# Edge stage on one core: counting every 16th key and gathering key groups, and the feed-forward output stored by channel

## The reference

```
h = (x_flat @ W_gat).reshape(M, HEADS, NUM_EXPERTS)
src = jnp.concatenate([edge_index[0], loops])
dst = jnp.concatenate([edge_index[1], loops])
e = jax.nn.leaky_relu(a_src[src] + a_dst[dst], negative_slope=0.2)
e_max = jax.ops.segment_max(e, dst, num_segments=M)
ee = jnp.exp(e - e_max[dst])
denom = jax.ops.segment_sum(ee, dst, num_segments=M)
alpha = ee / (denom[dst] + 1e-16)
msg = h[src] * alpha[:, :, None]
agg = jax.ops.segment_sum(msg, dst, num_segments=M)
...
for ei in range(NUM_EXPERTS):
    g = jnp.where(topk_i == ei, w, 0.0).sum(-1)
    hh = jax.nn.gelu(x @ W1[ei] + b1[ei], approximate=False)
    out = out + g[..., None] * (hh @ W2[ei] + b2[ei])
```

## Time and profile before

| | us |
|---|---|
| median of 3 runs | 5598.91 |
| lowest, highest | 5587.48, 5601.15 |
| profiled execution: span (the profile gives no other time of its own for it) | 6624.5 |
| first gather of the edge phase starts | 2448.2 |
| last gather starts | 6150.2 |
| finish phase starts | 6343.5 |

### The profile page before, as it was taken

How to read it: one execution, slowest core, us unless ns; L and a number is a source line. 1 busy time by engine, 2 the same in 40 slices (tenths; PEclk the granted TensorE clock), 3 DMA queues, 4 the chain that set the end, 5 groups by cost and what they waited for, 6 DMA issues and landing times. The chain is left out here.

```text
span 6624.5 us, 60648 instructions
## 1 busy us (share of the span) xinstructions
PE 3002.6 (45%) x16592; PEld 2109.7 (32%) x16592; DVE 3002.1 (45%) x4301; ACT 1456.9 (22%) x5679; POOL 2970.5 (45%) x3274
## 2 busy tenths in 40 slices
PE   2888888869999760000444241311313130130620
PEld 1445455458888650000233120200202120120410
DVE  5888888649999731010899120110101011010358
ACT  0334343348888510000000010000000000010110
POOL 1000000026667537777000657575675757667045
PEclk9788888769999855555555555555555555555555
DMA  6566556646666450000000011110111111011143
GB/s 141 87 95 96 94 94 95 95 75 102 101 104 103 87 146 8 8 7 8 3 3 3 10 37 25 34 28 14 45 15 34 25 34 28 14 45 15 58 166 118
DMA packets 583690, 381.06 MB, mean 58 GB/s; under 512 B 404996, under 2 KB 524852, under 8 KB 577748
## 3 DMA queue, kind: packets, MB, share of 16 engines
q1 hardware_dynamic: 384376, 216.58, 14.6%
q10 hardware_dynamic: 89403, 109.89, 9.4%
q0 software_dynamic: 109728, 52.69, 6.7%
HBM read 232.80 MB, written 145.29 MB: 57 GB/s over the span
## 5 line engine op out<-in xcount | busy, mean ns | idle before, releaser
L1569 POOL DMA_INDIRECT e_row<-scratch_table,e_edge x2048 | 2014.2, 983 | 989.2 <-issue 680.8
L1750 PE MATMUL f_psY<-f_w,f_hid 128*128 128x64 f32 x1568 | 363.0, 425 | 1657.4 <-ACT f_hid L1701 1292.2
L1633 DVE TENSOR_TENSOR f_y<-f_psY,f_b 128x1024 f32<-128x1024 f32 x49 | 59.8, 1219 | 2298.5 <-DMA scratch_t<-t 1711.2
L1750 PEld LDWEIGHTS f_psY<-f_w,f_hid 128*128 128x128 f32 x1568 | 342.5, 330 | 1753.4 <-ACT f_hid L1701 1371.8
L1608 DVE TENSOR_TENSOR i_hot<-f_psH,i_digit 128x1024 bf16<-128x1024 f32 x512 | 582.3, 1211 | 640.0 <-DMA scratch_parts<-h2p 356.8
L1701 ACT ACTIVATE f_hid<-f_psH,f_b 128x512 f32<-128x512 f32 x196 | 131.4, 687 | 2933.9 <-PE f_psH L1745 1351.7
L1733 PE MATMUL f_psH<-i_hot 128*128 128x128 bf16 x2048 | 264.8, 310 | 958.3 <-DVE i_hot L1608 761.2
L964 POOL MEMSET a_wproj<- 128x128 f32 x1 | 0.2, 210 | 1367.4 <-POOLq L161 1367.4
L1077 ACT ACTIVATE prob<-psS,low 128x100 f32<-128x100 f32 x1568 | 514.1, 373 | 61.9 <-DVE low L1110 61.9
L1733 PEld LDWEIGHTS f_psH<-i_hot 128*128 128x128 bf16 x2048 | 197.3, 140 | 1025.7 <-DVE i_hot L1608 825.7
L472 PE MATMUL psH<-h,c_w 128*128 128x448 f32 x1008 | 511.5, 595 | 3.8 <-ACT h L584 2.0
(11 more groups left out here) (281 smaller groups left out, 5329.9 us busy)
## 6 DMA issues: line engine op xcount, KB each, us to landing
stack<-scratch_parts ACTq DMA_DIRECT2D x504, 112.0 KB
e_row<-scratch_table,e_edge POOLq DMA_INDIRECT x2048
scratch_y<-f_y ACTq DMA_DIRECT2D x49, 512.0 KB
scratch_state<-e_state SPq DMA_DIRECT2D x16, 1536.0 KB, 6.0
g_y<-scratch_y SPq DMA_DIRECT2D x24, 1024.0 KB
val<-scratch_vpad SPq DMA_DIRECT2D x672, 35.0 KB
scratch_parts<-h2p ACTq DMA_DIRECT2D x56, 336.0 KB, 3.3
keys<-scratch_kpad SPq DMA_DIRECT2D x112, 155.0 KB
```

What stands on the lines that cost most here:

```text
L1569: pool.indirect_dma_start(out=row[s][:, f, :], out_offset=None, in_=table_dram, in_offset=bass.IndirectOffsetOnAxis(ap=edge[s][:, 0, f:f + ...
L1750: m = pe.matmul(psY[par][:, j, e * C:(e + 1) * C], hid[e][:, j * 128:(j + 1) * 128], w2[:, e, :], start=True, stop=True)
```

## The change

- **The count.** Only every 16th key of the sorted list is counted (`GROUP` = 16, 128 columns instead of 2048), which tells in which group of 16 keys a node's run ends. POOL then fetches that group for each node with 128 indirect DMAs of 16 keys (`group_keys`), and DVE compares the 16 keys with the node's number and adds up. `Index` writes 128 digit columns instead of 2048; `digit` shrinks from 2 MB to 128 KB.
- **The order on POOL.** Three chunks of gathers, the 128 key-group gathers, chunk 3, the run starts, then chunks 4 to 15. The store of the first elements moves from POOL to SP.
- **The ring.** Eight row buffers and edge buffers instead of four. The one-hot tiles lie in the eighth row buffer, the fetched keys in `part`, their floats in `state[0]`. All loops of the phase are written out.
- **The feed-forward.** The second layer loads the weights, widened with zeros to 128 columns, and streams the hidden tile: 4 matmuls of 512 columns per tile, two experts added in one PSUM bank half each. ACT moves the result out of PSUM with the bias, one tile behind the gelus, and it is stored by channel. DVE has no part in it. It starts when the base of the count is out of PSUM (`freed`). ACT's list has the exponential of chunk c behind tile `EXPS_AFTER[c]`.
- **The finish.** The slices come in by channel; PE turns them with 16 transposes each into PSUM (`g_psM`, two buffers), and DVE scales from there. The token loads have a semaphore of their own.

```diff
-AHEAD = 4
+AHEAD = 8
+KEYS_BEFORE, RUNS_BEFORE = 3, 4
+EXPS_AFTER = (14, 15, 16, 17, 18, 22, 25, 29, 33, 36, 40, 44, 47, 49, 49, 49)
...
-            dve.tensor_scalar(part_i[:], dst[:], 127, None, ALU.bitwise_and).then_inc(self.done, 1)
+            dve.tensor_scalar(group, lasts, 127, None, ALU.bitwise_and).then_inc(self.done, 1)
...
+                def group_keys():
+                    pool.wait_ge(grouped, 1)
+                    for t in range(128):
+                        pool.indirect_dma_start(out=keys[:, t, :], out_offset=None, in_=key_rows,
+                                                in_offset=bass.IndirectOffsetOnAxis(ap=group_ix[:, t:t + 1], axis=0)).then_inc(keys_in, 16)
...
+                for c in range(NFC):
+                    if c == KEYS_BEFORE:
+                        group_keys()
+                    if c == RUNS_BEFORE:
+                        first_of_run()
+                    gather(c)
...
+                dve.tensor_copy(group_ix[:], inc[:]).then_inc(grouped, 1)
+                done(dve.memset(base[:], 0.0))
+
+                dve.wait_ge(keys_in, 16 * 128)
+                done(dve.tensor_scalar(keys, keys, SRC_BITS, NODES - 1, ALU.logical_shift_right, ALU.bitwise_and))
+                done(dve.tensor_copy(keyf, keys))
+                dve.wait_ge(const_in, 48)
+                done(dve.tensor_tensor(keyf, keyf, node_id[:].unsqueeze(2).to_broadcast([128, 128, GROUP]), ALU.is_le))
+                done(dve.tensor_reduce(inside[:], keyf, AX.X, ALU.add))
...
+                def outputs(t):
+                    wait(act, y_out[t % 2], t // 2 * 16)
+                    for a in range(2):
+                        act.wait_ge(y_ready, t * 2 + a + 1)
+                        m = act.activation(y[t % 2][:, a, :], psY[t % 2][:, a, :], ACT.Identity, bias=b2[:, a:a + 1])
...
-                        for j in range(ZT // 128):
-                            m = pe.matmul(psY[par][:, j, e * C:(e + 1) * C], hid[e][:, j * 128:(j + 1) * 128], w2[:, e, :],
-                                          start=True, stop=True)
...
+                        m = pe.matmul(psY[par][:, e // 2, :], w2[:, e, :], hid[e][:], start=e % 2 == 0, stop=e % 2 == 1)
...
-                    dve.tensor_tensor(scaled[k % 2][:, 0:n], y[s][:, 0:n], gate[:, lo:hi, :].unsqueeze(3).to_broadcast([128, n, EXPERTS, C]),
+                    dve.tensor_tensor(scaled[k % 2][:, 0:n], psM[k % 2][:, 0:n], gate[:, lo:hi, :].unsqueeze(3).to_broadcast([128, n, EXPERTS, C]),
...
+                def turn(k):
+                    s, (lo, hi) = k % SLOTS, CHUNKS_AT[k]
+                    pe.wait_ge(y_in[s], loads(k))
+                    wait(pe, scale_done, k - 1)
+                    for j in range(hi - lo):
+                        for a in range(2):
+                            m = pe.transpose(psM[k % 2][:, j, 2 * a:2 * a + 2, :].rearrange("p e c -> p (e c)"),
+                                             y[s][:, a, j * 128:(j + 1) * 128], ident[:])
+                    m.then_inc(y_turned, 1)
```

More of the change, by code:

```diff
@@ L1227, in step @@
             dve.wait_ge(self.done, 5)
-            dve.tensor_copy(out[:, :, 5, :], chunks(part_i)).then_inc(self.digits, 1)
+            dve.tensor_copy(self.digit[:, 1, :], group).then_inc(self.digits, 1)
         elif i == 7:
@@ L1464, in edge_phase @@
         b_first = sb("e_b_first", [128, GHEADS])
[L1465 to L1468, removed]
+        iota = sb("i_iota", [128, 128]); before = sb("i_before", [128, 128]); node_id = sb("i_node_id", [128, 128])
+        digit = sb("i_digit", [128, 2, FC])
         zero = sb("i_zero", [128, 128], BF16)
@@ L1480, in edge_phase @@
         part = sb("e_part", [128, FC, GH])
-        w1 = sb("f_w1", [C, EXPERTS, 128]); b1 = sb("f_b1", [128, EXPERTS]); w2 = sb("f_w2", [128, EXPERTS, C])
-        b2 = sb("f_b2", [128, EXPERTS * C])
+        zeros = e0
+        keys = part[:].bitcast(I32)
+        keyf = state[0][:, :, 0:GROUP]
+        spare = row[AHEAD - 1][:].rearrange("p f c -> p (f c)").bitcast(BF16)
+        hot = [[spare[:, (2 * i + d) * HOT * 128:(2 * i + d + 1) * HOT * 128].rearrange("p (c x) -> p c x", x=128) for d in range(2)] for i in range(2)]
@@ L1527, in _ @@
                 for c in range(NFC):
[L1528 to L1532, removed]
+                    sp.dma_start(flat[c], zeros[:].rearrange("p f h -> p (f h)")).then_inc(b_zeroed, 16)
@@ L1537, in _ @@
+                sp.wait_ge(b_started, 16)
                 for par in range(2):
                     sp.dma_start(bsrc[par][:], b_view[par]).then_inc(b_in[par], 16)
[L1540 to L1556, removed]
+                for c in range(NFC):
+                    sp.wait_ge(scanned, c + 2)
+                    sp.dma_start(state_view[c], state[c % 2][:]).then_inc(state_out[c % 2], 16)
+                    if c + AHEAD < NFC:
+                        sp.dma_start(edge[c % AHEAD][:], edge_dram[c + AHEAD]).then_inc(edge_in[c % AHEAD], 16)
+                    if c + 2 < NFC:
+                        sp.dma_start(bsrc[c % 2][:], b_view[c + 2]).then_inc(b_in[c % 2], 16)
@@ L1724, in _ @@
+                for par in range(2):
+                    act.wait_ge(y_out[par], 16 * ((TILES_Z + 1 - par) // 2))
             @block.tensor
@@ L1814, in finish_phase @@
         of_slot = lambda k: range(k % SLOTS, k + 1, SLOTS)
[L1815 removed]
+        loads = lambda k: 16 * len(of_slot(k))
         stores = lambda k: 16 * sum(spans_of(*CHUNKS_AT[i]) for i in of_slot(k))
@@ L2053, in _ @@
                 m.then_inc(turned_back, 1)
+                pe.wait_ge(fix_limited, 1)
+                for k in range(1, NCH):
+                    turn(k)
             @block.scalar
@@ L2103, in host_layout @@
     out["ffn_b1"] = f(ffn("b1").T)
-    out["ffn_w2"] = f(ffn("W2").transpose(1, 0, 2))
-    out["ffn_b2"] = f(ffn("b2").reshape(1, EXPERTS * C))
+    w2 = np.zeros((128, EXPERTS, 2, C), np.float32)
+    for e in range(EXPERTS):
+        w2[:, e, e % 2, :] = ffn("W2")[e]
+    out["ffn_w2"] = f(w2.reshape(128, EXPERTS, 2 * C))
+    out["ffn_b2"] = f(ffn("b2").reshape(2, 2 * C).T)
     out["edges"] = f(ffn("edge_index"))
```

288 lines of the change are left out of this document (142 added, 146 removed).

## The result

| kernel | median us | lowest to highest | ratio to before, 95% interval |
|---|---|---|---|
| before | 5600.03 | 5587.48 to 5610.48 | |
| changed | 5722.36 | 5720.17 to 5728.25 | 1.0217 [1.0201, 1.0233] |

The changed kernel is 122 us slower; 110 were forecast (5709, range 5640 to 5752). All later kernels were timed against the kernel before on the same chip as they.

What follows compares the result with a forecast made beforehand. The prediction took POOL's issue of gathers to bound plain runs. Key groups +165, before chunk 4 -38, digits' store -5, tail -2 and finish -10 sum to +110, so 5599 + 110 = 5709 us, range 5640 to 5752.

Steps and rivals of the forecast that it cites:

- What bounds the kernel: Edge phase: POOL's issue of gathers bounds plain runs, at a pitch of 1.289 us; waiting for the count costs nothing there.
- the crawl: Other engines slowed beside gathers in the first profile (DVE 9 instructions in 100 us, otherwise 89); claimed absent from plain runs.
- Key groups: On POOL: 128 more indirect DMAs at 1.289 us each, covered by nothing, +165 us (160 to 168).
- The count at 0: On DVE: 480 one-hot tiles fewer, 540 us, gain nothing, as they already lie beside gathers.
- Before chunk 4: POOL's 38.40 us idle between scatters and chunk 4's gathers vanishes with eight buffers: -38 us, bounds 30 and 41.
- The digits' store: Before the edge phase: storing 128 KB of digits instead of 2048 KB saves 5 us, between 0 and 10.6.
- The feed-forward at 0: PE's second layer takes the same 7.1 us a tile in its new form, beside 1536 gathers: 0 us.
- The finish: After the edge phase: sums' waits shrink by at most about 25 us, transposes add; -10 us, ends -25 and +15.
- The rival in which each slice shows its transposes: In the finish, 25 slices each show a microsecond or two of transposes: +30 instead of -10, 5749 us; chance 0.09.
- The freed port: Rival: gathers speed up without DVE's one-hot tiles and evictions, 2048 x 0.02 = 40 us return, 5669; chance 0.08.
- The recording holds the other engines back: Chosen reading of the first profile: recording events slows other engines when they and gathers produce events together; plain runs have none.
- third reason: DVE's slowing sets in late after gathers resume at 3881.00: scans gap-free at 3961.63, idle from 3967.58, suggesting an event store filling.

Runs made afterwards that it cites:

- second recording of before: The kernel before, unchanged, profiled a second time: 5625.7 us in its one plain run, span 5624.1.
- sixteenth-count trace: The kernel before, counting only the first 128 of its 2048 columns (32 one-hot tiles instead of 512): ratio 0.9999 [0.9988, 1.0009].
- crawling recording: The first profile of the kernel before, unchanged, from which the prediction was made: span 6624.5 us, where the plain runs had a median of 5598.91.
- whole-count kernel: The changed kernel with the kernel before's count of all 2048 columns and no key groups: 5567.45 us, ratio 0.9933 [0.9911, 0.9956].
- doubled tiles: The kernel before, with DVE making a second, unused copy of every one-hot tile (1024 instead of 512): 6121.92 us, ratio 1.0918 [1.0900, 1.0936].

## Why the prediction was right, point by point

The terms, from the starts of POOL's instructions in the second recording of before (span 5624.1) and in that of the changed kernel (5726.7):

| stretch of POOL | before | changed | difference | forecast |
|---|---|---|---|---|
| start to first gather | 2460.6 | 2444.4 | -16.2 | -5 |
| gathers of chunks 0 to 3 | 652.3 | 653.0 | +0.7 | 0 |
| key groups | | 162.6 | +162.6 | +165 |
| `e_b_first`, scatters to the last one's start | 167.7 | 167.4 | -0.3 | 0 |
| last scatter to chunk 4 | 33.5 | 1.3 | -32.2 | -38 |
| chunks 4 to 15, to the last gather | 2004.5 | 2002.8 | -1.7 | 0 |
| last gather to finish | 25.8 | 24.6 | -1.2 | -2 |
| finish | 279.8 | 270.7 | -9.1 | -10 |
| sum | | | +102.6 | +110 |

Measured were 122, and most of the gap of 19 to 102.6 lies in the one recording of before: it is 17 us above the median of the other runs on its chip (5625.7 against 5608.7). With the sixteenth-count trace in its place (span 5606.7; a kernel of the same time) the difference is 120.0. Start to first gather then gives -10.7, chunks 0 to 3 +2.3, before chunk 4 -31.7, chunks 4 to 15 +6.5, the way to the finish -0.9 and the finish -8.1; key groups and scatters stay. So a row of the table is good to 5 or 10 us (chunks 4 to 15 alone take 1998 to 2007 in five recordings of the changed kernel and of variants that don't touch them), and only the key groups and the wait before chunk 4 stand far above that. That 110 came within 12 of 122 rests on these two, 162.6 for 165 and some -32 for -38; that the small terms fit as well is partly luck.

- **What bounds the kernel** held. That the stalls of the earlier trace rows weren't in the plain runs was argued from the stretched stretches and from a sum without free terms; the second recording and the sixteenth count show it. Taken at their word, those rows had promised a gain of hundreds of us. The prediction's other sentence, that POOL's gathers and their pitch were not touched by the crawl, was wrong: chunks 0 to 3 took 692.1 us there and 652.3 in the second recording. So some 40 of the 60 us that it left to "the mean pitch" came from the crawl.
- **Key groups**: 162.6 against 165, and no byte has a share in it.
- **The count at 0** held, with a cover of 60 to 64 us; 1.12 us a tile had given about 63 (3088 - 3025).
- **Before chunk 4**: right in mechanism, 6 us too much, the only miss that stands clear of the spread. The row for it came from the crawling recording, in which DVE came to the run starts 7.9 us later than in the second one (11.1 us after their load's issue against 3.2). Each step of a cost taken from a disturbed trace has to be looked at for the disturbance.
- **The digits' store** was sized right (from its issue to the edge phase 30.2 us with 2 MB in the sixteenth-count trace, 23.5 in the changed kernel's), where -5 was forecast. The rest of the -16.2 lies ahead of that store, and it is spread: the four recordings with the kernel before's front part reach the store between 2415.3 and 2427.2 us, and the whole-count kernel, which has the 2 MB and their work back, reaches it at 2413.1, before the changed one (2418.1).
- **The feed-forward at 0** held: in the changed kernel its last tile is stored at 4951, 500 us before the last scans end. That its second layer would take the same 7.1 us a tile did not hold. It was busy for 214.0 us in 49 tiles against 347.3, 4.4 a tile. The mean granted clock over the stretch was 0.56, where it had been 0.50, the lower of the two levels, all along; the first layer, whose instructions are as before, took 184.6 us for 352.4. So no run tells what the new form alone is worth.
- **The finish**: -9.1 is in the main the sum of two that pull apart. DVE's waits for sums fell by 19.0; its waits for turned slices are 21.2 where those for loads were 13.3. The rival in which each slice shows its transposes didn't come.
- **The Trainium skill, SBUF — State Buffer, § SBUF: two separate sides** says that a DVE operation with two SBUF inputs and a reading GpSimd operation exclude each other. 164.2 us of sums' gathers against 141.7, with nothing changed but where an input lies, agree. That the whole 25 us would come back was too much: POOL's gathers got 20.3 of them (162.0 to 141.7), DVE's waits for the sums 19.0, and the kernel's finish 9.1, as the slices' waits took the rest.
- **The freed port** as a rival for the gathers: out. The pitch of chunks 1 to 3 is 1.271 in the sixteenth count, without one-hot tiles, and 1.271 beside the doubled ones. Those tiles read one input from PSUM. That of chunks 5 to 15 is 1.30 with DVE's evictions of the feed-forward (sixteenth count) and without (changed kernel). It is the scans' stage that lifts it to that.
- **"The recording holds the other engines back"** isn't shown. That crawl was in one recording of eleven here, was absent from a second one of the same program and from one with more instructions (61160, the doubled tiles). Nor does the prediction's third reason, the late onset, hold for the first stage. DVE's first six one-hot tiles run without a gap, and the idle stretches begin 11 us after the first gather (2448.22):

```profile
2452.37 6.88 DVE L1608 TENSOR_TENSOR i_hot<-f_psH,i_digit 128x1024 bf16<-128x1024 f32 x6 [7.39 <-issue]
2465.59 2.36 DVE L1608 TENSOR_TENSOR i_hot<-f_psH,i_digit 128x1024 bf16<-128x1024 f32 x2 [6.34 <-DMA scratch_parts<-h2p]
2483.22 2.35 DVE L1608 TENSOR_TENSOR i_hot<-f_psH,i_digit 128x1024 bf16<-128x1024 f32 x2 [15.27 <-issue]
```

What the prediction needed of it, that the plain runs have no crawl, is shown; no run tells what caused it.

## What to carry to other kernels

When a profile's span is far above the plain runs, first find the stretch that is stretched and rebuild the plain time from the rows that aren't; a second recording is the cheapest experiment of all. An indirect DMA of 128 rows had a fixed price on the engine that issues it, 1.27 us here: replacing 480 vector instructions that are hidden by 128 such DMAs on the engine that is never idle is a loss, whatever it saves in work. And of a change in several parts, the parts should be priced on the bounding engine one by one: here three gained and one lost more than all of them.

## What the runs showed of the hardware

- An indirect DMA of 128 rows takes POOL 0.94 us and 0.30 us until the next, for rows of 4, 64 or 80 bytes, gather or scatter alike (0.98 for a scatter). Once in 128 the idle time before one is 2.9 us longer, which makes the mean pitch 1.270.
- A DVE product with both inputs in SBUF holds up one gather that meets it (beside the changed kernel's products of 2.27 us, 2.96 us in twelve chunks and 3.37 in three, instead of 0.94); several in a row let one gather through each, at 2.33 us a piece. Beside a chunk's scans most gathers take no more than 1.2.
- One recording of a program can hold long waits (532 us, seven of up to 53.7) that neither its plain runs nor its next recording have. The engine that looked undisturbed in it, POOL, was slowed too (a gather of 1.07 us for 0.94).
